# Mamba and expert block on one core: GpSimd folds the output weights and adds the bias, and one product of B is placed ahead of a projection of z

## The reference

```
h  = layernorm(x) * (1 + ca) + sa
x1 = x + ga * mamba(h)          # scan over 1024 tokens, 512 channels, 16 states
h2 = layernorm(x1) * (1 + cb) + sb
out = x1 + gb * experts(h2)     # 8 experts, the best 2 of each token

mamba(h): B = h WB', C = h WC', delta = softplus(...), u = silu(conv(h Wx' + bx))
          z = h Wz' + bz
          s[t] = exp(delta*A) * s[t-1] + (delta*u) * B[t];   y[t] = sum over states of s[t]*C[t]
          y = (y + u*D) * silu(z);   return y Wout' + bout
```

## Time and profile before

| | us |
|---|---|
| median of 3 runs | 813.56 |
| lowest and highest | 810.22 and 817.89 |
| profiled execution, its time | 814.6 |
| its span in the profile | 812.8 |
| PE busy | 710.9 (87%) |
| DVE busy | 616.8 (76%) |
| GpSimd busy | 515.3 (63%) |
| ACT busy | 370.2 (46%) |

### The profile page before, as it was taken

The page is one execution under the profiler, slowest core; times in us unless marked ns, Lnnn a source line. Parts: engine busy times, 40 slices in busy tenths (PEclk is TensorE's granted clock), DMA queues, the critical chain, the costliest instruction groups (busy, mean ns, idle before and its releaser), DMA issues. The chain is left out here.

```text
span 812.8 us, 10546 instructions
## 1 busy us (share of the span) xinstructions
PE 710.9 (87%) x3018; PEld 426.0 (52%) x3019; DVE 616.8 (76%) x818; ACT 370.2 (46%) x415; POOL 515.3 (63%) x271
## 2 busy tenths in 40 slices
PE   5799999888688786887898887999699999999993
PEld 3444443323233232322443533347699999999993
DVE  4478888999999899999999999897454445445441
ACT  1778776445644454444544557431212333333330
POOL 1012223799999999999999999896653333333232
PEclk9999999999999999999999999999599999999997
DMA  9364733877776767667687997877584332333220
GB/s 287 93 175 139 217 147 96 200 198 168 183 180 174 191 160 187 185 172 197 177 222 214 267 246 169 250 185 258 163 262 88 54 53 41 53 51 48 44 31 0
DMA packets 62302, 126.47 MB, mean 156 GB/s; under 512 B 11898, under 2 KB 33850, under 8 KB 62140
## 3 DMA queue, kind: packets, MB, share of 16 engines
q1 hardware_dynamic: 50468, 116.12, 52.9%
q0 software_dynamic: 7152, 8.48, 6.1%
q10 hardware_dynamic: 4648, 1.48, 0.8%
HBM read 98.08 MB, written 24.69 MB: 151 GB/s over the span
## 5 line engine op out<-in xcount | busy, mean ns | idle before, releaser
L1720 POOL TENSOR_TENSOR pool<-pool,hT 128x1024 f32<-128x1024 f32 x92 | 214.8, 2356 | 15.1 <-PE PS L705 15.0
L1087 ACT ACTIVATE PS<-pool,negA 128x1024 f32<-128x1024 f32 x128 | 143.0, 1118 | 174.6 <-DVE pool L1410 174.6
L705 PE MATMUL PS<-pool,ident 128*128 128x512 f32 x368 | 185.3, 628 | 32.5 <-POOL pool L1720 31.8
L1807 POOL DMA_INDIRECT out<-uT,ptab x39 | 61.6, 1580 | 132.4 <-DMA out<-uT,ptab 69.4
L1410 DVE TENSOR_TENSOR_SCAN pool<-PS,pool 128x1024 f32<-128x1024 f32 x64 | 143.1, 2273 | 0.4 <-ACT PS L1087 0.4
L705 PEld LDWEIGHTS PS<-pool,ident 128*128 128x128 f32 x368 | 68.2, 196 | 109.3 <-POOL pool L1720 52.4
L921 PE MATMUL PS<-uT,hT 128*128 128x128 f32 x992 | 115.8, 274 | 0.0
L921 PEld LDWEIGHTS PS<-uT,hT 128*128 128x128 f32 x992 | 113.3, 192 | 0.1
L687 PE MATMUL PS<-pool 96*128 96x512 bf16 x256 | 79.3, 392 | 28.3 <-DVE pool L1398 14.9
L1720 POOL TENSOR_TENSOR Y<-pool,hT 128x1024 f32<-128x1024 f32 x36 | 84.0, 2358 | 2.8 <-PE PS L705 2.8
L1744 POOL TENSOR_TENSOR spread<-spread,pool 128x1024 f32<-128x1024 f32 x32 | 75.4, 2355 | 13.7 <-ACT spread L1093 13.5
(11 more groups left out here) (207 smaller groups left out, 921.4 us busy)
## 6 DMA issues: line engine op xcount, KB each, us to landing
hT<-C_scratch SPq DMA_DIRECT2D x128, 512.0 KB, 5.4
pool<-in_w SPq DMA_DIRECT2D x16, 512.0 KB, 7.3
uT<-expert_in_scratch SPq DMA_DIRECT2D x39, 130.5 KB, 2.1
Y<-Y SPq DMA_DIRECT2D x32, 128.0 KB, 2.4
C_scratch<-Y SPq DMA_DIRECT2D x8, 512.0 KB, 2.6
pool<-du_scratch SPq DMA_DIRECT2D x8, 512.0 KB, 6.2
Y<-in_wo SPq DMA_DIRECT2D x8, 512.0 KB, 7.4
expert_in_scratch<-zrow SPq DMA_DIRECT2D x16, 130.5 KB, 6.4
```

Of the source, the lines that this page charges most:

```text
L705: m = pe.matmul(PS[:, 6 + half, :], ident[:, :], prod_k[:, HF * half:HF * half + HF], start=False, stop=k == DS - 1)
L1087: act.activation(pair(2 * (k % 2)).unsqueeze(1), delta[:, chunk_at(g2, r), :], ACT.Exp, scale=decay[:, bass.ds(g2 * (2 * DS) + n, 1)]).the ...
L1720: gp.tensor_tensor(to, hst[:, k % HR, :], crep[k % RC], ALU.mult).then_inc(prod_done, 1)
L1807: gp.indirect_dma_start(out=out, out_offset=bass.IndirectOffsetOnAxis(ap=ptab[:, slot:slot + 1], axis=0), in_=yo[:, slot % RY, :], in_offs ...
```

## The change

It makes three edits. First, the folding of the output weights and the adding of the bias leave DVE, where they stood behind the projections, and go to GpSimd: the two folds and the bias of batch 0 behind the product du of chunk 3, the bias of batch 1 behind that of chunk 5. Secondly, PE spreads the first B (`front(0, 0, 0)`) after z of chunk 4 instead of after z of chunk 5. Thirdly, since this lets ACT start its exponentials before z of chunk 5 is out, chunk 5 joins chunks 6 and 7: it is taken out without silu (`keep_z`), and `late_silu` covers three chunks instead of two.

```diff
@@ TensorE
-            for n in range(NG - 2):
+            for n in range(NG - 3):
                 z_of(n, 2 * (n % 2))
...
             front(0, 0, 0)
+            z_of(NG - 3, 2 * ((NG - 3) % 2))
             z_of(NG - 2, 6)
             front(0, 0, 1)
             front(0, 0, 2)
@@ ScalarE
-            for n in range(NG - 2):
+            for n in range(NG - 3):
                 act.wait_ge(z_mm, n + 1)
                 act.activation(szT[:, n, :], pair(2 * (n % 2)), ACT.Silu, bias=...).then_inc(sz_done, 1)
...
-            act.wait_ge(sz_done, 2 + NG - 2)
+            act.wait_ge(sz_done, 2 + NG - 3)
             act.wait_ge(du_made, NG)
...
             def late_silu():
                 act.wait_ge(sz_done, 2 + NG)
-                act.activation(szT[:, NG - 2:NG, :], szT[:, NG - 2:NG, :], ACT.Silu).then_inc(sz_done, 1)
+                act.activation(szT[:, NG - 3:NG, :], szT[:, NG - 3:NG, :], ACT.Silu).then_inc(sz_done, 1)
...
                         decays(g2, r, k)
                         if first and r == 0 and k == 0:
+                            keep_z(NG - 3)
+                            act.wait_ge(sz_done, 2 + NG - 2)
+                        if first and r == 0 and k == 1:
                             keep_z(NG - 2)
@@ VectorE
-            dve.tensor_tensor(wout0[:, :, :], wout_sb[:, :, :], ga[0].broadcast_to([P, CH, DM]), ALU.mult).then_inc(folded, 1)
-            dve.wait_ge(folded, 1)
-            dve.tensor_tensor(wout_sb[:, :, :], wout_sb[:, :, :], ga[1].broadcast_to([P, CH, DM]), ALU.mult).then_inc(folded, 1)
-            dve.wait_ge(folded, 2)
-            for b in range(NB):
-                mine = x_tok[:, NTB * b:NTB * b + NTB, :]
-                dve.tensor_tensor(grow[:, b, 0, :], grow[:, b, 0, :], row, ALU.mult).then_inc(bout_done, 1)
-                dve.wait_ge(bout_done, 2 * b + 1)
-                dve.tensor_tensor(mine, mine, ga[b].broadcast_to([P, NTB, DM]), ALU.add).then_inc(bout_done, 1)
@@ GpSimd
+            def wout_folded():
+                gp.wait_ge(w_in, 16 * (2 + CH))
+                gp.wait_ge(grow_in, 16 * (1 + 2 * KD))
+                gp.tensor_tensor(wout0[:, :, :], wout_sb[:, :, :], ga[0].broadcast_to([P, CH, DM]), ALU.mult).then_inc(folded, 1)
+                gp.wait_ge(folded, 1)
+                gp.tensor_tensor(wout_sb[:, :, :], wout_sb[:, :, :], ga[1].broadcast_to([P, CH, DM]), ALU.mult).then_inc(folded, 1)
+                gp.wait_ge(folded, 2)
+
+            def bout_added(b):
+                mine = x_tok[:, NTB * b:NTB * b + NTB, :]
+                gp.tensor_tensor(grow[:, b, 0, :], grow[:, b, 0, :], row, ALU.mult).then_inc(bout_done, 1)
+                gp.wait_ge(bout_done, 2 * b + 1)
+                gp.tensor_tensor(mine, mine, ga[b].broadcast_to([P, NTB, DM]), ALU.add).then_inc(bout_done, 1)
...
                 gp.tensor_tensor(du_st[g % 2], delta[:, delta_at(g), :], uT[:, g, :], ALU.mult).then_inc(du_made, 1)
+                if g == CH - 1:
+                    wout_folded()
+                    bout_added(0)
+                if g == CH + 1:
+                    bout_added(1)
```

More of the change, by code:

```diff
@@ L1110, in keep_z @@
                     act.wait_ge(du_out[1], 16 * (NG // 2))
-                act.activation(szT[:, n, :], pair(6), ACT.Identity, bias=col[:, BZ + n % CH:BZ + n % CH + 1]).then_inc(sz_done, 1)
+                act.activation(szT[:, n, :], pair(6 if n >= NG - 2 else 2 * (n % 2)), ACT.Identity, bias=col[:, BZ + n % CH:BZ + n % CH + 1]).then_inc(sz_done, 1)
             def late_silu():
                 act.wait_ge(sz_done, 2 + NG)
-                act.activation(szT[:, NG - 2:NG, :], szT[:, NG - 2:NG, :], ACT.Silu).then_inc(sz_done, 1)
+                act.activation(szT[:, NG - 3:NG, :], szT[:, NG - 3:NG, :], ACT.Silu).then_inc(sz_done, 1)
             def decays_of(g2, first):
@@ L1377, in _ @@
                 delta_of(3)
-            dve.wait_ge(w_in, 16 * (2 + CH))
-            dve.wait_ge(grow_in, 16 * (1 + 2 * KD))
-            ga = [grow[:, b, 0, :].unsqueeze(1) for b in range(NB)]
-            dve.tensor_tensor(wout0[:, :, :], wout_sb[:, :, :], ga[0].broadcast_to([P, CH, DM]), ALU.mult).then_inc(folded, 1)
-            dve.wait_ge(folded, 1)
-            dve.tensor_tensor(wout_sb[:, :, :], wout_sb[:, :, :], ga[1].broadcast_to([P, CH, DM]), ALU.mult).then_inc(folded, 1)
-            dve.wait_ge(folded, 2)
-            for b in range(NB):
-                mine = x_tok[:, NTB * b:NTB * b + NTB, :]
-                dve.tensor_tensor(grow[:, b, 0, :], grow[:, b, 0, :], row, ALU.mult).then_inc(bout_done, 1)
-                dve.wait_ge(bout_done, 2 * b + 1)
-                dve.tensor_tensor(mine, mine, ga[b].broadcast_to([P, NTB, DM]), ALU.add).then_inc(bout_done, 1)
             def drive(g2, r, k):
@@ L1457, in added_y @@
                 dve.wait_ge(o_mm, t + 1)
+                if t == NTB:
+                    dve.wait_ge(bout_done, 2 * NB)
                 dve.tensor_tensor(x_tok[:, t, :], PS[:, o_bank(t), 0:DM], x_tok[:, t, :], ALU.add).then_inc(x2_step, 1)
@@ L1693, in _ @@
                 gp.tensor_tensor(rstd[:, half], rstd[:, half], nhalf[:, half], ALU.pow).then_inc(rstd_done, 1)
+            ga = [grow[:, b, 0, :].unsqueeze(1) for b in range(NB)]
+            def wout_folded():
[10 more added lines that the diff above has]
+                gp.tensor_tensor(mine, mine, ga[b].broadcast_to([P, NTB, DM]), ALU.add).then_inc(bout_done, 1)
             for g in range(NG):
```

## The result

The changed kernel took **820.69 us** (median of 4 runs, 819.77 to 823.0) against 812.93 of the kernel before in the same comparison (median of 4), a ratio of 1.0085 [1.0052, 1.0117]. The ratio is time over the time before, with its 95% interval. It is slower by 7 to 8 us, a little under 1%, and the interval is clear of no change. The forecast was 820.0, in a range of 812 to 824.

The account below looks back on a forecast made before the run. PE was taken to set the pace until 134 us, with DVE close behind, and DVE to bound the scan. Delays of 6.0 and 0.8 less 0.41 gave +6.4: 813.56 + 6.4 = 820.0 us, range 812 to 824.

Parts of the forecast that it names:

- the ends of a held-up operation: DVE beside GpSimd: a blocked DVE operation ends 1.08 us after GpSimd's, a blocked fold 2.2 after DVE's.
- The roundings, the one kind no row showed: DVE's two scalar_tensor_tensors after C of chunk 0: wait for the addition, 6.0 us late; if not held up, sum 4.1.
- How it reaches PE: PE waits for DVE's late copies of C: 2.7 us late, then 6.0 up to z of chunk 0.
- The 0.41 at the second front: PE's idle time before the second front: all the earlier scan start gained from 9.9 us taken off DVE.
- the term at z: At z of chunk 2: second addition delays one_plus, ln and silu, so PE starts 0.7 to 0.8 us later.
- Late silu and clock: In the scan: silu 0.96 us longer on ACT, taken as 0; clock effects of -1.7 and +1.0 kept for the range.
- The low clock that the forecast feared: Behind PE's second idle time: C of chunk 2 some 1.7 us longer, 0.7 covered; +1.0 kept for the range.
- the favourable case: At z of chunk 7: clock stays at 2.4 GHz with one idle time left, so 1.7 us come back; range only.
- No loss: Rival: finer port sharing or additions falling into DVE's pauses, 813.2 to 811.5 us; chance 0.15.
- GpSimd keeps DVE out for its whole chain: Rival: DVE's subtraction for B waits from 85.8 to 95.6 us, scan 9.2 late, so 823; chance 0.12.
- A gain of over 1% from the earlier front: Rival: the scan gains from the earlier front in an unseen way, over 1% faster; chance 0.03.
- The forecast's mechanism: Before the scan: GpSimd's work holds DVE up for 4 to 8 us, giving 817.5 to 821.5; chance 0.70.

Follow-up runs that it names:

- fourth kernel: The change, with the bias back on DVE behind the projections and only the two folds on GpSimd: 815.72 us, ratio 1.0034.
- eighth kernel: The change, with folds, small products and batch 0's bias on DVE from 35 us, batch 1's bias on DVE behind the projections: 812.34 us, ratio 0.9990.
- second kernel: The kernel before, with the first front ahead of z of chunk 5 and three chunks in late_silu; folds and bias stay on DVE: 814.3 us, ratio 1.0001.
- third kernel: The kernel before, with 15 memsets of 128x1024 on GpSimd where the change has its folds and additions: 813.57 us, ratio 0.9999.
- tenth experiment: The change itself, timed again against the kernel before: 821.2 us, ratio 1.0104.

## Why the prediction was right

- **What bounds the kernel, and the ends of a held-up operation.** Right. The subtraction was to end at 89.2 and ended at 89.07, one_plus at 91.9 (91.83), the third part of B at 93.6 (93.50).
- **The roundings, the one kind no row showed.** They were to be 6.0 late and are 5.7 late, judged by the copy of C behind them: 103.81 against 98.17, and the 0.10 by which the subtraction is earlier. Taking them like a tensor_tensor was right: 5.53 for two beside the addition, 2.34 for two with no addition beside them (fourth kernel) and beside memsets. The Trainium skill's rule (SBUF — State Buffer, "Who interferes with whom"), that two SBUF inputs contend with a GpSimd instruction that reads SBUF and not with one that only writes it, agrees on both sides: 5.53 beside the addition, 2.34 beside memsets.
- **How it reaches PE.** C of chunk 2 at 105.4 forecast, 105.08 measured; z of chunk 0 at 115.2 and 114.79; z of chunk 2 at 122.8 and 122.34 behind 0.52 of waiting for the silu; second front at 140.6 and 140.05. The waits for copies of C are seen in both executions and in the kernel with GpSimd's work alone.
- **What is removed.** The 0.41 at the second front is nearly the whole value of a freed DVE: -0.6 with the work done elsewhere (eighth kernel), and no difference in time.
- **The sum.** +6.4 forecast; +5.95, +5.98 and +5.96 in the two profiles of the change and the one of GpSimd's work alone, counted from the subtraction for B. Of the 0.4 to 0.5 between them, 0.3 lie in the roundings (5.7 for 6.0) and the rest in the wait at z of chunk 2 (0.52 for 0.7 to 0.8). The small products were estimated at 0.6; one that nothing held up took 0.73. The additions, estimated at 4.6, took 4.51. One step does not add up: the second addition was said to end at 118.7, where the forecast's own terms give 112.9 + 0.6 + 4.6 = 118.1. It ended at 118.22. With 118.1 the term at z would have been nearly nothing and the sum 5.6 to 5.7, so that this slip stood in for the second small product, which took 1.18 and not 0.6.
- **The number.** 820.69 measured for 820.0 is closer than the forecast deserves. The median of the kernel before was 812.93 in the comparison and not 813.56, and the loss was 7.8 us and not 6.4.
- **Late silu and clock.** The silu of three chunks took 2.77 (2.87 forecast), with no cost in time (second kernel). The low clock that the forecast feared behind PE's second idle time came behind the first: C of chunk 1 began after 3.34 us of idle time, at a granted clock of 0.50 between 95 and 97 us, and took 5.08 instead of 3.70. It cost nothing, since PE then waited for the copy of C of chunk 1 anyway, 1.88 us. z of chunk 7 kept the high clock, 3.60 us instead of 5.30, as the favourable case had it, and it did not help: the fifth front waited for ACT in its place, as these rows of TensorE, of ScalarE and of the clock after show.

```profile
148.79 1.03 PE L687 MATMUL PS<-pool 96*128 96x512 bf16 x2 [2.27 <-ACT Y L1112]
```

```profile
146.41 1.12 ACT L1088 ACTIVATE PS<-pool,negA 128x1024 f32<-128x1024 f32 x1 [1.06 <-DVE pool L1400]
147.46 1.09 ACT L1112 ACTIVATE Y<-PS,col 128x1024 f32<-128x1024 f32 x1
```

```profile
148.70:152.10 3.40, 3.31 (x5) 1.48 (x6) 3.40 (x3) 1.12 (x1) 2.12 (x1) 0.50 1.01 228
```

The fifth front waits 2.27 us for the plain copy of z of chunk 7 (`keep_z`). Its place in ACT's list is the same in both kernels, behind the exponential of the fourth state. Before, z of chunk 7 ended after that exponential and the copy followed z. Now z ends first, at 146.10, and the copy follows the exponential, which itself waits 1.06 us for DVE's scan. The low clock, which had been at 138 us, comes here. What z of chunk 7 gave (-1.7, +4.2 at the third and fourth scan) was gone by the fifth (+5.8). The prediction had not named this wait; it had kept the clock's gain in the range only.

Its condition for the high clock, one idle time of PE instead of two, is not borne out. With the memsets (third kernel) PE has both idle times, and z of chunk 7 takes 3.60 all the same; with the front moved alone (second kernel), behind 0.40 and 1.41, it takes 4.97. The case came true, its reason is not shown.

```profile
134.48 0.61 PE L687 MATMUL PS<-pool 96*128 96x512 bf16 x2 [0.97 <-DVE pool L1399]
136.49 0.60 PE L687 MATMUL PS<-pool 96*128 96x512 bf16 x2 [1.41 <-DVE pool L1399]
136.94 3.60 PE L598 MATMUL PS<-hT,wz_sb 128*128 128x512 f32 x8
```

- **The rivals.** No loss: excluded, the roundings did not keep their time. GpSimd keeps DVE out for its whole chain: excluded, the subtraction lasted 3.36 and not 10, so the two take turns. A gain of over 1% from the earlier front: not seen (1.0001 with the front moved alone). The forecast's mechanism stands.
- **The measured loss** is 7 to 8.5 us by the two ratios (0.0085 and 0.0104 of 813), with lower ends of 4.2 and 6.7; the start of the scan accounts for 6.0. By the estimate under the tenth experiment about 1 us of the rest goes with a lower mean clock of those runs. Why their clock is lower, and whether some tenths are left beyond that, stays open.

## What to carry to other kernels

Idle time of GpSimd is free for elementwise work only where DVE has no instruction at hand that reads two inputs from SBUF, nor a tensor_scalar from SBUF to SBUF. Elsewhere such work holds DVE up for as much as its own length; here 15.7 us on GpSimd made DVE's other operations about 10 us longer. Cutting the additions in eight won back 1.3 of the 6.0 us at the start of the scan, an earlier place on GpSimd 2.8, and neither made the work free. Before work is moved off an engine, look for the wait that ends last in front of the next stage (0.41 us here, of 9.9 moved), and for idle time of the same engine earlier in the program: DVE did the same work in half the time at 35 us, for nothing. And with DVE out of the way, the gain is in moving what its lateness had held back (here the second front), not in the move itself.

## What the runs showed of the hardware

- Beside memsets of GpSimd, which read nothing, tensor_tensor and scalar_tensor_tensor keep their length (1.23 us, and 2.34 for two), but a tensor_scalar of float32 in SBUF is held up (1.47 against 0.69 us). A memset of 128x1024 takes 1.05 us, a tensor_tensor of that size on GpSimd 2.35.
- The same kernel's scan lasted 4.5 us more in one execution than in another (410.2 and 405.6 us from the first scan to the last), with stretches at the lower clock in different places. A term of the sum smaller than that can't be read from the end of one profile. The start of the scan repeats within 0.6, and within 0.03 when it is counted from an operation just ahead of the change.
- The time of a run goes with its mean granted clock: 3.1 us for each 0.01 here.
